# The long filter of the first attention: all 64 taps on VectorE instead of 52 on VectorE and 12 on GpSimd (POOL)

## The reference, cut to what matters

```
short[c, t] = sum over j in 0..4  of fir_short_w[c, j] * v[c, t - 4  + j]
long[c, t]  = sum over j in 0..63 of fir_long_w[c, j]  * v[c, t - 63 + j]
```

## Time and profile before

| | |
|---|---|
| runs | 6267.53, 6274.35, 6282.97 us (median 6274.35) |
| the profiled execution | 6270.57 us, its span 6269.3 us |
| busy, share of the span | PE 66%, PEld 50%, DVE 54%, ACT 31%, POOL 17% |
| first attention | from the start to about 1.3 ms, four rounds that repeat within some us, 319.0 us apart (L1271 of lane 0 at 255.1, 574.1, 893.7, 1212.6) |
| L1212, VectorE taps | 440 instructions, 360.6 us busy in all |
| L1376, L1378, L1373, GpSimd taps | 184 instructions, 254.5 us busy in all |

### The profile page before, as it was taken

One profiled execution on the slowest core, in us unless ns is written; L12 is line 12 of the kernel. 1 busy time (PEld: TensorE's weight loads), 2 busy tenths in 40 slices (PEclk: granted clock), 3 DMA queues, 4 the chain that ended last, 5 costly groups with the idle time before them and its releaser, 6 DMA issues.

```text
span 6269.3 us, 101968 instructions
## 1 busy us (share of the span) xinstructions
PE 4154.9 (66%) x43020; PEld 3112.6 (50%) x43020; DVE 3389.1 (54%) x8405; ACT 1946.1 (31%) x4228; POOL 1068.6 (17%) x784
## 2 busy tenths in 40 slices
PE   3746465656787787884646656566666777667298
PEld 2535353535555555553535445454444554445277
DVE  7575767633555545556355554646656555555332
ACT  2232222212333333330232232324444444443122
POOL 4040404023111101111600000001111111110433
PEclk6555555558889889985766666667778887778599
DMA  9000000014000000001210000000000000000155
GB/s 259 4 1 1 1 2 1 2 59 138 1 1 1 1 1 1 1 1 33 30 35 2 2 1 2 1 2 1 1 1 1 1 1 1 1 1 1 62 152 142
DMA packets 140747, 148.62 MB, mean 24 GB/s; under 512 B 7792, under 2 KB 127986, under 8 KB 139776
## 3 DMA queue, kind: packets, MB, share of 16 engines
q1 hardware_dynamic: 118880, 124.04, 6.8%
q0 software_dynamic: 21408, 18.05, 1.7%
HBM read 83.21 MB, written 59.76 MB: 23 GB/s over the span
## 4 chain that ended last, share of the span: by engine, by line
PE 44%; DVE 37%; ACT 10%; issue 5%; POOL 2%; DMA 1%; another core or an unknown queue 1%; SPq 0%; DVEq 0%; POOLq 0%; ACTq 0%
ACT work L3175 3%; PE banks_lane L422 3%; DVE weights L1212 3%; DVE work L1212 2%; PE banks_lane L3612 2%; PE banks_lane L1831 2%; PE banks_lane L3017 2%; PE banks_lane L3061 2%; PE banks_lane L935 1%; DVE weights L3268 1%; ACT work L1925 1%; PE banks_lane L3096 1%; PE banks_lane L793 1%; DVE work L2738 1%; PE banks_lane L3083 1%
## 5 line engine op out<-in xcount | busy, mean ns | idle before, releaser
L422 PE MATMUL banks_lane<-constants,work 128*128 128x128 f32 x920 | 189.4, 353 | 446.5 <-DVE work L408 194.0
L402 POOL TENSOR_TENSOR weights<-weights,constants 128x4 f32<-128x4 f32 x80 | 82.7, 1034 | 2057.9 <-DVE weights L397 2057.9
L422 PE MATMUL banks_lane<-constants,weights 128*128 128x128 f32 x612 | 131.1, 358 | 424.4 <-DVE weights L408 134.3
L422 PEld LDWEIGHTS banks_lane<-constants,work 128*128 128x128 f32 x920 | 144.0, 182 | 513.6 <-DVE work L408 184.4
L3175 ACT ACTIVATE work<-banks_lane,weights 128x192 f32<-128x192 f32 (+1 forms) x512 | 248.5, 499 | 245.6 <-DVE weights L3272 245.6
L422 PEld LDWEIGHTS banks_lane<-constants,weights 128*128 128x128 f32 x612 | 95.4, 184 | 449.4 <-issue 169.9
L3280 POOL TENSOR_TENSOR weights<-weights,constants 128x16 f32<-128x16 f32 x64 | 185.5, 2898 | 530.7 <-DVE weights L3188 530.7
L402 POOL TENSOR_TENSOR work<-work,constants 128x4 f32<-128x4 f32 x72 | 73.4, 1020 | 1180.6 <-DVE work L397 1180.6
L3096 PE MATMUL banks_lane<-constants,work 128*128 128x128 f32 x896 | 149.7, 316 | 120.3 <-DVE work L3260 70.7
L1978 DVE TENSOR_REDUCE work<-banks_lane 128x2 f32<-128x512 f32 x256 | 158.8, 683 | 67.9 <-PE banks_lane L1845 67.4
L3096 PEld LDWEIGHTS banks_lane<-constants,work 128*128 128x128 f32 x896 | 113.3, 160 | 150.1 <-DVE work L3260 89.2
(11 more groups left out here) (807 smaller groups left out, 11677.3 us busy)
## 6 DMA issues: line engine op xcount, KB each, us to landing
work<-experts_dram_l_ffn SPq DMA_DIRECT2D x39, 964.0 KB
room_l_ffn<-work SPq DMA_DIRECT2D x30, 1188.0 KB, 13.9
work<-experts_dram_l_ffn SPq DMA_DIRECT2D x23, 512.0 KB
weights<-weights_dram SPq DMA_DIRECT2D x1, 4833.5 KB, 14.4
work<-room_l_ffn SPq DMA_DIRECT2D x36, 132.0 KB
weights<-weights_dram SPq DMA_DIRECT2D x1, 4112.0 KB, 12.4
weights<-room_l_ffn SPq DMA_DIRECT2D x26, 132.0 KB
weights<-weights_dram SPq DMA_DIRECT2D x1, 3378.0 KB, 10.8
```

Source lines behind the costliest of these rows:

```text
L402: pool.tensor_tensor(n.rstd, n.rstd, c("neghalf", cols=(0, n.rstd.shape[1])), ALU.pow).then_inc(*u.pool.step(name))
L422: done = pe.transpose(bank[0:rows, t * P:(t + 1) * P], block, c("ident"))
```

## The change

GpSimd gets no tap, VectorE takes all 64 of the long filter. `tap_pool`, the two buffers of GpSimd and the final sum on VectorE go away. 69 taps instead of 57 are spread over the same 26 slots, by another rule for the yields (3, 2, 3, 3, 2, 3 and so on). The mark `filtered`, for which TensorE waits before the turns, is now the last tap.

```diff
-L0_ATTN_POOL_TAPS = 12
...
-        self.shortT, self.longT, self.poolT, self.product = (arena.take(SEQ) for _ in range(4))
+        self.shortT, self.longT = (arena.take(SEQ) for _ in range(2))
...
-        taps += [("long", m.longT, L0_ATTN_LONG, j) for j in range(L0_ATTN_POOL_TAPS, L0_ATTN_LONG)]
+        taps += [("long", m.longT, L0_ATTN_LONG, j) for j in range(L0_ATTN_LONG)]
...
-                dve.scalar_tensor_tensor(dst, window, factor, dst, ALU.mult, ALU.add).then_inc(*u.dve.step())
-            if n % 11 in (1, 3, 5, 7, 10):
+                dve.scalar_tensor_tensor(dst, window, factor, dst, ALU.mult, ALU.add).then_inc(*u.dve.step("filtered"))
+            if n % 8 in (2, 4, 7):
                 yield
...
         for _ in filters:
             pass
-        dve.wait_ge(*u.pool.at("filtered"))
-        dve.wait_ge(*u.dve.last())
-        dve.tensor_tensor(m.longT, m.longT, m.poolT, ALU.add).then_inc(*u.dve.step("filtered"))
         yield "branches"
...
-        tap = 0
         for pair in range(CHUNKS // 2):
-            for phase in delta_phases(pair):
-                if phase.startswith("left"):
-                    self.tap_pool(pool, u, tap)
-                    tap += 1
-                yield phase
+            yield from delta_phases(pair)
```

More of the change, by code:

```diff
@@ L1364, in pool @@
             yield phase
[L1366 to L1378, removed]
 def stage_l0_attn(run, w, arena, X):
```

## The result

| | before | after |
|---|---|---|
| median of six runs | 6272.2 us (6262.5 to 6289.6) | 6217.7 us (6214.4 to 6232.3) |
| profiled execution | 6270.6 us | 6220.5 us |
| its span | 6269.3 us | 6219.2 us |
| VectorE busy | 3389.1 us | 3349.0 us |
| GpSimd busy | 1068.6 us | 818.8 us |

The changed kernel is faster: ratio 0.9913, 95% interval 0.9898 to 0.9929. Forecast were -43 us; measured are -50.1 between the two profiled executions and -54.5 between the medians. VectorE has 96 taps more and 8 sums less, and yet is busy for 40 us less.

The account below looks back on a forecast made before the run. VectorE's queue was taken to set the pace in both pairs. Added taps +66, stalls returned -101 and end sum -8 gave -43 us, from a median of 6274.35 to 6231 us, range 6214 to 6262.

Parts of the forecast that it names:

- The price of a tap: VectorE's slots in both pairs: each added tap that is seen costs 0.79 us, without GpSimd beside it.
- Which taps are seen: Both pairs: 21 of 24 added taps a round are seen, 16.5 us a round, +66 us in four.
- the slack: Lane 1's L912 after the first pair: 2.07 us before TensorE takes its product, covering 1.57 us of added delay.
- What the stalls give back: First pair 17.9 us (from the second pair's 58.85), preparation 7.4: together 25.3 a round, -101 us in four.
- The end sum: Lane 1's L1271 behind lane 0's statistics holds TensorE's turns; without it 1.9 us a round, -8 us (-2 to -14).
- Rival 3: TensorE's granted clock changes here or in a later stage: about 15 us either way, 6216 or 6246; chance 0.10.
- rival 1: Preparation keeps its length, ScalarE or TensorE being its limit; the statistics' 1.9 also lost: -6 us, 6268; chance 0.07.
- rival 2: First pair is slow for a reason that stays, GpSimd not the cause: 58 us slower, 6332; chance 0.05.

Follow-up runs that it names:

- the first version with GpSimd between the pairs: Changed kernel with 6 long-filter taps of each unit back on GpSimd, started after the unit's last tap of the first pair: 6211.3 us, ratio 0.9902.
- the memsets: Changed kernel plus 23 GpSimd memsets of 128x512 floats in place of its tap instructions, writing SBUF and reading none: 6211.6 us, ratio 0.9912.
- the dead taps: Changed kernel with GpSimd doing its 12 taps again into a buffer that nobody reads, without the end sum: 6320.4 us, ratio 1.008.

## Why the prediction was right

- **The price of a tap, 0.79 us**, is what the second pair shows: 7.9 us for 10. The estimate of 0.69 from the Trainium skill, VectorE: DVE Perf Modes, "The TRN2 errata", would have given 6.9; the trace shows 0.75 us of duration for one tap, and 0.04 more until the next, which needs it, can start.
- **Which taps are seen.** Three of 24 were forecast as hidden. 8.9 + 7.9 = 16.8 us a round were measured against 16.5, and 65 in all by the ends of the stage in the two traces, as the run without GpSimd's taps has one first pair of 59.1. Lane 1's L912 did come 5.2 us behind lane 0's instead of 3.8, and the recurrence stayed at 24.4, so the slack held; when more was put there (7.8 us, the first version with GpSimd between the pairs) it broke.
- **What the stalls give back**, 17.9 in the first pair and 7.4 in the preparation: 75.1 - 57.1 = 18.0 and 42.9 - 35.5 = 7.4. (The terms that the prediction takes from 58.85 give 18.1 to 18.6, not 17.8 to 18.6; the 17.9 that it chose was closer by luck.) Both directions of it were run, away and back, and the changed kernel's first pair (forecast 65.9, measured 66.0), second pair (66.8, 66.7) and preparation (35.5, 35.5) came out by it.
- **The end sum**, forecast 1.9 a round within 0.6 to 3.4: 1.4 or 1.9 by the run that moved it alone, at the clock of that run. The mechanism, TensorE's queue held by a sum that stood behind the other lane's statistics, is as put.
- **What was short**: -43 forecast, -50 in the profiled execution, of which 48.5 lie in this stage. The term that was not in the sum is the clock. The end stretch shrank by 1.4 us in two rounds and by 5.6 in two; with the end sum moved alone it is 60.1 in all four, so the 3.5 to 3.8 from there to 56.6 and 56.4 are TensorE at 0.56 instead of 0.50. Rival 3 had named a clock that answers, with a shift of 15 us to either side, and placed it nowhere. Here it gave 7.3 us. The other 1.6 us of the -50 arose behind the stage, and that they are so few is luck: in the run with the end sum moved the unchanged stages shifted by 12 to 17 us. The medians' -54.5 is within what the interval allows (-45 to -64).
- VectorE's wait before the sums of lane 0, by which rival 1 was to show itself, is 5.76 us before and after. Rival 1 (preparation) and rival 2 (GpSimd not the cause) are excluded by the run without GpSimd's taps, rival 2 also by the run that put them back.

## What to carry to other kernels

Work that is given to GpSimd to relieve VectorE is not free for VectorE: compare the mean duration of the same instruction in stretches with and without GpSimd, by operand (two inputs in SBUF, one, or PSUM), before counting on the split; here 46 instructions a round cost VectorE's path 25 us and saved it 17. Where GpSimd should have such work, hand it over in the stretches in which VectorE waits for others, with a wait that keeps it there, since a queue without one runs ahead into the busiest part. And a combining operation at the end of an in-order queue is to be priced by what it stands behind, not by its duration.

## What the runs showed of the hardware that was not expected

- GpSimd's memsets of 128x512 floats (0.53 us) do not slow VectorE's two-input operations by a measurable amount (lane 1's convolution taps, some of them beside nine memsets, 751 to 754 ns in all rounds, 750 to 752 in the changed kernel; L871 414 ns with and without), its `tensor_tensor` of the same size does (VectorE's taps 926 to 948 ns as a mean over a stretch that it half fills, L871 1264). A `tensor_scalar` beside a memset took 0.81 us instead of 0.36.
- VectorE's reduces (0.69 us) and transposes (445 ns), with one input in SBUF, were as fast beside GpSimd's `tensor_tensor` as without it.
- TensorE's mean granted clock in the end stretch was 0.56 in some rounds and 0.50 in others, 56.4 against 60.1 us, while no round of the kernel before took under 61.5 (60.1 with the end sum moved). In the first profile it came in the second and fourth round, in the next in the first and third. Rounds whose end is shorter by such a spell (3 us or more) are found in the profiles of all kernels in which GpSimd's taps do not run through preparation and first pair (the changed one, the one without taps, the memsets, and those with taps in the gaps), and in none of the three in which they do, the dead taps among them (60.1 in all four). The kernel before has a clock of 0.53 there, but its spells fall between the statistics (0.86 and 0.71 in the 6 us from 595), where TensorE is idle for more than half of the time. So part of what that run lost against the changed kernel, 7 of 112 us by the stage's end, is the clock and not VectorE's stalls. That is one execution of each kernel; what decides it stays open, and no run here was made for it.
- Between kernels that differ only in the first attention the unchanged stages drift by 12 to 17 us against each other, which is as much as the smaller effects here; the stretches of the trace, which agree within 0.1 us, told them apart where the medians could not.
